# First K by load steps, V's weights ahead of the chunks, and two of the first four looks on GpSimd, in a fused cross-attention and FFN kernel

## The reference

```python
def attention(ctx, xn, mask):                 # 32 batches, 128 positions
    k, v = split((ctx @ W_src.T + b_src) * mask)          # 512 -> 2 x 256
    q = (xn @ W_tgt.T + b_tgt) * mask                     # 256 -> 256
    p = softmax(where(mask == 0, -inf, q @ k.T / sqrt(32)))    # 8 heads of 32
    return concat(xn, p @ v) @ W_out.T + b_out
def ffn(xn):                                  # w1, w2, h1, h2, w3 hold -1, 0, 1
    h = silu((xn @ w1.T) * s1) * ((xn @ w2.T) * s2)       # 256 -> 1024
    h = gelu((h @ h1.T) * sh1)                            # 1024 -> 1024
    h = gelu((h @ h2.T) * sh2)
    return (h @ w3.T) * s3                                # 1024 -> 256
x = x + attention(ctx, layernorm(x), mask)
x = x + ffn(layernorm(x))
```

## Time and profile before

| | |
|---|---|
| runs | 921.73, 923.12, 924.48 us; median 923.12 |
| profiled execution | 924.39 us, span 922.6 us |
| PE busy | 909.7 us, 99% of the span |
| VectorE, ScalarE, GpSimd busy | 614.3, 387.4, 75.3 us (67%, 42%, 8%) |
| chain that ended last | PE 90%, DMA 3%, VectorE 2%, ACT 2% |

### The profile page before, as it was taken

The page is one execution under the profiler, slowest core; times in us unless marked ns, Lnnn a source line. Parts: engine busy times, 40 slices in busy tenths (PEclk is TensorE's granted clock), DMA queues, the critical chain, the costliest instruction groups (busy, mean ns, idle before and its releaser), DMA issues.

```text
span 922.6 us, 20860 instructions
## 1 busy us (share of the span) xinstructions
PE 909.7 (99%) x7604; PEld 867.7 (94%) x7604; DVE 614.3 (67%) x1217; ACT 387.4 (42%) x1095; POOL 75.3 (8%) x101
## 2 busy tenths in 40 slices
PE   8999999999999999999999999999999999998998
PEld 7889999999999999999999999999999999998998
DVE  4886758568574876757667585785758768566353
ACT  5682523535343352523525244343533526254231
POOL 3434001010000100001010000100001000000000
PEclk9999999999999999999999999999999999999999
DMA  8922132312223122132311323122131221212000
GB/s 327 374 93 81 36 120 69 119 46 70 80 60 119 57 75 83 41 119 68 97 57 38 116 68 119 46 74 79 57 119 57 87 75 37 91 36 92 24 12 14
DMA packets 82347, 79.20 MB, mean 86 GB/s; under 512 B 8976, under 2 KB 74896, under 8 KB 82320
## 3 DMA queue, kind: packets, MB, share of 16 engines
q1 hardware_dynamic: 82320, 78.84, 26.5%
HBM read 51.55 MB, written 27.26 MB: 85 GB/s over the span
## 4 chain that ended last, share of the span: by engine, by line
PE 90%; DMA 3%; DVE 2%; ACT 2%; SPq 1%; issue 1%; POOL 0%; DVEq 0%; ACTq 0%; POOLq 0%
PE F L585 55%; PE G L578 6%; PE F L689 6%; PE G L585 6%; PE G L447 5%; PE G L480 5%; PE G L465 2%; PE S L496 2%; PE G L561 2%; DMA p_dram<-pb 1%; DMA WV<-wv 1%; SPq L313 1%; PE F L480 1%; ACT pr L829 1%; DMA pr<-p_dram 1%
## 5 line engine op out<-in xcount | busy, mean ns | idle before, releaser
L801 ACT ACTIVATE g<-F,scols 128x256 f32<-128x256 f32 x256 | 107.1, 471 | 333.0 <-PE F L585 332.8
L585 PE MATMUL F<-hAh,H 128*128 128x256 f32 x1024 | 243.0, 282 | 1.6 <-ACT g L801 0.8
L585 PE MATMUL F<-hBh,H 128*128 128x256 f32 x1024 | 243.5, 282 | 0.1
L585 PE MATMUL F<-hAl,H 128*128 128x256 f32 x1024 | 240.6, 279 | 0.0
L585 PE MATMUL F<-hBl,H 128*128 128x256 f32 x1024 | 240.6, 279 | 0.0
L585 PEld LDWEIGHTS F<-hAh,H 128*128 128x128 f32 x1024 | 192.2, 188 | 4.6 <-ACT g L801 1.2
L585 PEld LDWEIGHTS F<-hBl,H 128*128 128x128 f32 x1024 | 192.7, 188 | 0.4
L585 PEld LDWEIGHTS F<-hBh,H 128*128 128x128 f32 x1024 | 192.3, 188 | 0.6 <-ACT g L801 0.3
L585 PEld LDWEIGHTS F<-hAl,H 128*128 128x128 f32 x1024 | 192.7, 188 | 0.0
L1136 DVE CAST hBh<-g 128x512 fp32r<-128x512 f32 x64 | 28.1, 439 | 140.6 <-ACT g L801 140.5
L829 ACT ACTIVATE pr<-pr,nmx 128x128 f32<-128x128 f32 x256 | 98.9, 388 | 1.9 <-DVE nmx L1013 1.7
(11 more groups left out here) (138 smaller groups left out, 1451.4 us busy)
## 6 DMA issues: line engine op xcount, KB each, us to landing
p_dram<-pb SPq DMA_DIRECT2D x30, 512.0 KB, 3.4
pr<-p_dram SPq DMA_DIRECT2D x120, 128.0 KB, 2.5
H_raw<-h SPq DMA_DIRECT2D x16, 512.0 KB, 11.8
cT<-ctx_t SPq DMA_DIRECT2D x15, 512.0 KB, 3.4
x_dram<-xt SPq DMA_DIRECT2D x28, 256.0 KB, 2.3
out<-y SPq DMA_DIRECT2D x32, 128.0 KB, 1.8
x_in<-x_t SPq DMA_DIRECT2D x15, 256.0 KB, 2.7
x2T<-x_dram SPq DMA_DIRECT2D x60, 64.0 KB, 1.9
```

The lines of the kernel that those rows point to most:

```text
L585: return mm(bank, W[0][:, k, cols], part[:, k, :], start=first, stop=last)
L801: fn(g[:, q % 2, m, :], F[q % 2][:, m, :], ACT.Gelu, scale=scols[:, col:col + 1]).then_inc(gelu_ready, 1)
```

## The change

The first tile's K is accumulated over its four load steps. Step k of WK (issued by ACT) and step k of cT (issued by SP) raise one semaphore, k_step_loaded[k], and both halves of K advance by one step, the second half in bank F1 instead of G1. This stands ahead of the transposes of x, and the warm-up has 4 products in place of 10. WV is issued ahead of the first four chunks. The looks at chunks 2 and 3 move from ACT to GpSimd, where they, mask_bv and the sum now stand ahead of the four casts. VectorE masks both batches' scores before it counts the low bits. The arithmetic is the same.

```diff
-WARM = 10
+WARM = 4
+        def k_bank(a, c):
+            return f_bank(1)[:, 0:T] if isinstance(a, int) and a == 0 and c == 1 else G[1][:, c * T:(c + 1) * T]
-        on_act = [0, 1, 2, 3, 4, 5, 7, 10, 11, 12, 13, 14, 15, 16, 17, 18, 20, 21]
+        on_act = [0, 1, 4, 5, 7, 10, 11, 12, 13, 14, 15, 16, 17, 18, 20, 21]
         on_dve = [6, 19]
-        on_pool = [8, 9]
+        on_pool = [2, 3, 8, 9]
...
             sp.dma_start(x_in[:], x[0]).then_inc(x_loaded, 16)
-            sp.dma_start(cT[:], ctxT[0]).then_inc(ctx_loaded, 16)
-            sp.dma_start(WK[:], wsT).then_inc(wk_loaded, 16)
+            for k in range(KC):
+                sp.dma_start(cT[:, k, :], ctxT[0][:, k * T:(k + 1) * T]).then_inc(k_step_loaded[k], 16)
...
+            sp.dma_start(WV[:], wvT).then_inc(wv_loaded, 16)
             load_chunks(range(EARLY))
-            sp.dma_start(WV[:], wvT).then_inc(wv_loaded, 16)
...
+            def project_k_0():
+                for k in range(KC):
+                    pe.wait_ge(k_step_loaded[k], 32)
+                    for c in range(KD):
+                        ins = mm(k_bank(0, c), WK[:, k, c * P:(c + 1) * P], cT[:, k, :], start=k == 0, stop=k == KC - 1)
+                        if k == KC - 1:
+                            ins.then_inc(k_done, 1)
...
+            project_k_0()
             transposes_x(0)
-            project_k(0, 0)
-            project_k(0, 1)
             project_q(0)
...
+            for k in range(KC):
+                act.dma_start(WK[:, k, :], wsT[:, k, :]).then_inc(k_step_loaded[k], 16)
             act.wait_ge(consts_ready, 2)
             fn(act_set[:], neg_half[:, 0:1], ACT.Exp).then_inc(act_set_ready, 1)
             copy_xnT(0)
             keep_xnT(0)
-            look(on_act[:4])
+            look(on_act[:2])
...
             mask_scores(0, 0)
             row_max(0, 0)
+            mask_scores(0, 1)
+            row_max(0, 1)
             count_low_bits(0, EARLY)
-            mask_scores(0, 1)
             raise_flag(0)
-            row_max(0, 1)
             normalise(0, 0)
...
             inverse_std1(0)
+            for n in on_pool[:2]:
+                look(n)
+            mask_bv()
+            sum_low_bits(0)
             for n in range(EARLY):
                 cast(n)
-            sum_low_bits(0)
-            mask_bv()
             pool.wait_ge(probs_ready, at("probs_ready", 0, 1))
             add_bias(0)
```

More of the change, by code:

```diff
@@ L222, in program @@
         act_set_ready = sem("act_set_ready")
-        wk_loaded = sem("wk_loaded")
+        k_step_loaded = [sem(f"k_step_loaded{k}") for k in range(KC)]
         wq_loaded = sem("wq_loaded")
@@ L264, in wait_ctx @@
         def wait_ctx(engine, a):
-            if isinstance(a, int) and a == 1:
+            if isinstance(a, int) and a == 0:
+                for k in range(KC):
+                    engine.wait_ge(k_step_loaded[k], 32)
+            elif isinstance(a, int) and a == 1:
                 engine.wait_ge(ctx_loaded_1, 16)
             else:
-                engine.wait_ge(ctx_loaded, 16 if isinstance(a, int) and a == 0 else at("ctx_loaded", a - 1, 16))
+                engine.wait_ge(ctx_loaded, at("ctx_loaded", a - 2, 16))
         def wait_mrow(engine, a):
@@ L437, in transposes_x @@
                 ins.then_inc(xt_done, 1)
+            def project_k_0():
[5 more added lines that the diff above has]
+                            ins.then_inc(k_done, 1)
             def project_k(a, c):
-                pe.wait_ge(wk_loaded, 16)
                 wait_ctx(pe, a)
@@ L446, in project_k @@
                 for k in range(KC):
-                    ins = mm(G[1][:, c * T:(c + 1) * T], WK[:, k, c * P:(c + 1) * P], cT_of(a)[:, k, :],
+                    ins = mm(k_bank(a, c), WK[:, k, c * P:(c + 1) * P], cT_of(a)[:, k, :],
                              start=k == 0, stop=k == KC - 1)
@@ L884, in tile @@
                     if first:
-                        look((on_act[6:7], on_act[7:9], [], on_act[9:15])[q])
+                        look((on_act[4:5], on_act[5:7], [], on_act[7:13])[q])
                 if first:
                     copy_xnT(2)
-                    look(on_act[15:])
+                    look(on_act[13:])
                 if a is not None:
@@ L916, in _ @@
             copy_upd_0(1)
-            look(on_act[4:5])
+            look(on_act[2:3])
             copy_xnT(1)
@@ L922, in _ @@
             x2_hi_0(1)
-            look(on_act[5:6])
+            look(on_act[3:4])
             tile(0, 1, 2)
@@ L971, in bias_mask_k @@
                 for c in range(KD):
-                    V.scalar_tensor_tensor(kT[:, c, :], G[1][:, c * T:(c + 1) * T], bcols[:, c:c + 1],
+                    V.scalar_tensor_tensor(kT[:, c, :], k_bank(a, c), bcols[:, c:c + 1],
                                            mrow_of(a), ALU.add, ALU.mult).then_inc(kT_ready, 1)
@@ L1354, in _ @@
             pool.wait_ge(x2_ready, at("x2_ready", 0, 2))
-            for n in on_pool:
+            for n in on_pool[2:]:
                 look(n)
```

## The result

The changed kernel takes 930.12 us, median of four runs (929.42 to 933.19), against 923.6 us for the kernel before: 6.5 us slower, ratio 1.008 (95% interval 1.0056 to 1.0104). The forecast was 926.9 in a range of 924.5 to 929.3. The direction was right, the size was not, and the time lies above the range.

A forecast was written before the change was run, and what follows sets the result against it. PE, busy 99% of the span, was taken to bound the kernel. 2.15 us (GpSimd's late casts) plus 1.6 us (lower clock) gave +3.75 us on the median 923.12: 926.9 us, range 924.5 to 929.3.

The forecast's parts named there:

- What bounds the kernel: Whole kernel: PE, busy 99%, bounds it; a delay in the first 35 us delays the end.
- Two looks on GpSimd: Before P's transposes: GpSimd's casts come last, the fourth ending at 24.8, so the transposes start 2.15 us later than 22.65.
- DVE's new order: VectorE before P's transposes: normalise(0, 0) by 22.5 and V's bias by 23.4, ahead of 24.8; cost nothing, bound 2 us.
- K by steps: Tile 0's start: K ends at 8.3 (7 to 11), scores start near 12.3, 1.0 us sooner (bounds -0.7 and +2.1).
- the clock rises late at the start: Rival at the start: after four warm-up products K runs at half clock, scores 0.7 us later; 928.9 us, chance 0.14.
- The clock: PE's restart at P's transposes: lower clock after 3.8 us of standing still costs 1.6 us (bounds 0 and 3.6).
- The sum: Whole kernel: 2.15 for the later transposes plus 1.6 for the lower clock, +3.75 us.
- WV sooner: V in tile 0: WV lands near 10.6, V follows the scores at 13.4 to 17.0; its earlier end returns nothing.
- The second queue: Loads at the start: ACT's queue adds no rate and earns only issue time that was hidden; the sum stays the same.

The follow-up runs named there:

- e2: Kernel before with only the GpSimd part (looks at chunks 2 and 3, mask_bv and sum ahead of the casts) and the changed VectorE order; ratio 1.0046.
- e3: Changed kernel with the four casts also waiting for batch 0's probabilities, so no cast runs beside normalise(0, 0); ratio 1.0087 to the kernel before.
- e1: Changed kernel with the GpSimd part undone: looks at chunks 2 and 3 back on ACT, casts first again; ratio 1.0033 to the kernel before.
- e5: Changed kernel plus 26 unread identity products on PE between tile 1's first half of K and the flag's read; ratio 1.0037 to the kernel before.
- e10: Kernel before with one edit, the warm-up cut from 10 products to 4; ratio 1.0029 to the kernel before.
- e4: Changed kernel with one edit, the warm-up back at 10 products instead of 4; ratio 1.0066 to the kernel before.
- e11: Changed kernel with WK's four steps issued by SP, each behind cT's, so ACT issues no transfer; ratio 1.0088 to the kernel before.
- e7: Kernel before with one edit, WV issued ahead of the four chunks; ratio 1.0006 to the kernel before.
- e12: e6 with WK's steps issued by SP instead of ACT; ratio 1.0033 to the kernel before.
- e8: e1 with a warm-up of 8 products and the transposes of x ahead of K's last step; ratio 1.0011 to the kernel before.
- e6: e1 with the warm-up back at 10 products; ratio 1.0015 to the kernel before.
- e9: e8 with the look at chunk 3 alone on GpSimd ahead of its cast, and 8 idle products between V and tile 1's K; ratio 1.0016.

## Why the prediction was wrong

**What bounds the kernel**: right. The gate to the transposes of P was where it was decided, and what was lost there and behind it is the 6.5 us of the median.

**Two looks on GpSimd**: right in mechanism and prices. Looks began at 14.42 (14.7 said), took 3.91, the casts 3.98 in a row. The end of the casts was 25.80 and not 24.8, for the reason in the next two steps.

**DVE's new order**: this is the step that failed. It said of normalise(0, 0): "That runs by 22.5 and V's bias by 23.4, both ahead of 24.8: nothing." It began at 22.29 and ran until 26.88, because this VectorE product, with both inputs in SBUF, did not get through beside back-to-back casts. That makes P's start the last cast's end plus 1.2 us: the price of one whole multiply, which the sum had hidden under the casts. The prediction had the sign of this in hand, the 1.34 us mask_bias beside a look in rows 5, and applied it to the negated maximum alone, as one instruction that waits for one other. e2 (4.64 us) and e3 (1.22 us) show what holds it. The Trainium skill's "GPSIMD Engine Reference", section "1. Specifications", says that GpSimd's way into SBUF is shared with VectorE, with contention for VectorE instructions with two SBUF inputs. The traces agree: 4.59 us beside the casts, 1.22 without. There is no gain from the other order, as e3 shows (0.6 us dearer); what else would help, casts that are done earlier for one, was not tried.

**K by steps**: "I take 8.3" for K's end was 10.33, and in e3, e1 and e5 9.7, 11.2 and 11.5; K also began at 4.90, after 1.22 us of waiting for its first step, and not at 4.0 to 4.5. By the records' durations the clock rose between 7.5 and 11 us in the kernels with the warm-up of 4, where it had risen at about 5.5 in the kernel before. The rival "the clock rises late at the start" had this with 0.14; it happened in every kernel with the warm-up of 4, to a different degree in each. So the scores came 1.3 us later than before and not 1.0 sooner, the count at 21.3 and not 19.1, and GpSimd's sum waited for it: 1.0 us in the end. e10 gives the price of that one number by itself, 0.29%.

**The clock** behind the gap: mechanism right, size off. 1.6 was taken and 2.6 measured (14.73 - 12.14), with V's 1.8 us as the measure. V was at work for the whole of its slow stretch; here PE worked from 26.99 to 32.6 at half speed, 5.6 us in place of 3.4. The size varies between executions: behind gaps of 5.60, 5.77 and 6.43 us (e4, e11, e3) the same measure gives 1.9, 1.9 and 2.1 us. The bounds 0 and 3.6 held. e5 shows the cause by taking it away.

**The sum** by its steps: 2.15 said for P's start, 4.34 measured, of which 1.0 is the late count, 1.2 the held multiply; 1.6 said behind it, 2.6 measured. The terms that were put at nothing are 2.2 of the 3.2 us by which the forecast's 3.75 falls short of this trace's 6.9 at the gate product. On the medians it falls short by 2.8 (6.5), and the kernel before was itself 0.5 us slower than the 923.12 that the forecast stood on.

**WV sooner**: right. V ran at full clock directly behind the scores (3.72 us) and this was worth nothing in the changed kernel, and by itself no more than 0.1 us at the gate product (e7).

**The second queue**: the step held that ACT's queue earns only issue time, which is hidden. The first half fits the runs: the Trainium skill's rule in "DMA: Bandwidth & Descriptors", section "Issuing engines are not separate DMA queues", is that only issue time is saved, and e11's delay of 1.6 to 1.7 us agrees with 1.90 us of later issues. The second half does not: with transfers of 128 KB the issues were not under a backlog, for in e11 the DMA share was 0.77 and 0.80 at 3 to 5 us, in place of 0.98 and 0.99. The changed kernel does issue WK on ACT, so this cost the forecast nothing.

**The range** was too narrow because its upper end was one rival's sum. It took the late rise to 928.9 without a held multiply. The late rise happened, with a late count and more time at the lower clock behind, and its 5.75 us with the multiply's 1.2 give the trace's 6.9.

**Left open**: PE waits 1.0 to 2.0 us for P's way in tile 0 in all ten kernels with K by steps, and 0.5 to 0.7 in the four without. The writes of P take longer there (4.67 and 3.86 us in the changed kernel, 3.35 and 2.99 before). It isn't ACT's queue (e11, e12), and nothing else was tried. It is about 1 us, as much as e8 gains at the front.

## What to carry to other kernels

When work moves to GpSimd, list what VectorE runs beside it: a product of two SBUF inputs beside a run of GpSimd casts costs the rest of the run plus its own time, so it counts as queued behind the run, not beside it. A gap that PE is put into costs its length plus half of the slow stretch behind it, here 1.9 to 2.6 us behind 5.6 to 6.4 of standing still and 1.5 to 1.6 behind 2.2 to 2.8. A warm-up is judged by where the records show the clock to rise. A wait that is moved to just ahead of the critical step brings the lower clock with it (e6). And when two late inputs meet at one instruction, price each of them as the last one before either is put at nothing.

## What the runs showed of the hardware

- VectorE's multiply with two inputs in SBUF beside four casts on GpSimd: 4.59 to 4.64 us in five kernels, 1.22 without them. Beside other work of GpSimd it was free: 1.22 beside mask_bv in e1, where mask_bv's second half took 1.49 in place of 0.91. Mask_scores (one input in PSUM) took 1.23 beside casts and beside looks.
- VectorE's negated maximum (128x8), 0.17 us alone, took 0.69 and 0.67 (e9) and 0.90 (e12) beside a cast and ended within 0.02 us of the cast's end each time; beside two looks it took 1.86 in e11 and 0.39 in e3.
- By the records' durations the clock rose at about 5.2 to 7 us with ten warm-up products and at 7.5 to 11.3 with four, in other places in kernels that are the same up to there (7.5 in e3, 11 in e5).
- A second slow stretch lies near the end, between 850 and 870 us, in six of the fourteen profiled executions. In the kernel before, PE waits 1.8 us for P's way, and the clock is at its lower level just behind. Its windows:

```profile
850.00:852.00 2.00, 0.16 (x8) 0.07 (x8) 1.12 (x2) 0.45 (x2) 0.00 (x0) 1.00 0.43 122
...
852.00:854.00 2.00, 2.00 (x19) 1.44 (x20) 0.00 (x0) 0.60 (x1) 0.00 (x0) 0.56 0.00 0
...
854.00:856.00 2.00, 2.00 (x7) 1.59 (x7) 0.00 (x0) 0.00 (x0) 0.00 (x0) 0.59 0.00 0
```

In the other eight (e1, e4 to e8, e10 and e12) the clock is 1.00 from 840 to 870 us, though e10 and e12 wait longer there, 2.4 and 2.6 us. So the length of this wait alone does not decide it. By the windows above it costs some 1.7 us when it comes (an estimate: half of the 3.4 us at 0.50 that they amount to), and it may be part of the kernel's own scatter from run to run (921.73 to 924.48); that was not tested.
